# Mamba on one core: the products that add dt*u*B for half of TensorE's pairs of states become scalings on ScalarE and transposes

## What is computed

```python
xz = h @ in_proj_w
u, z = jnp.split(xz, 2, axis=-1)
u = silu(causal_depthwise_conv(u, conv_w, conv_b))
xdbl = u @ x_proj_w                      # dt_r, B, C
dt = softplus(dt_r @ dt_proj_w + dt_proj_b)
A = -jnp.exp(A_log)
def step(hst, inp):
    dt_t, B_t, C_t, u_t = inp
    dA = jnp.exp(dt_t[..., None] * A)
    dBu = dt_t[..., None] * B_t[:, None, :] * u_t[..., None]
    hst = dA * hst + dBu
    y = jnp.einsum('bdn,bn->bd', hst, C_t)
    return (hst, y)
y = (scanned y + u * D) * silu(z)
out = x + y @ out_proj_w
```

## Time and profile before

| | us |
|---|---|
| median of 3 runs | 2734.17 |
| lowest and highest run | 2731.04, 2740.05 |
| profiled execution | 2753.53 |
| its span | 2751.6 |
| busy in the span: PE, DVE, ACT, POOL | 2466.9, 2244.3, 1961.6, 1899.4 |

### The profile page before, as it was taken

How to read it: one execution, slowest core, us unless ns; L and a number is a source line. 1 busy time by engine, 2 the same in 40 slices (tenths; PEclk the granted TensorE clock), 3 DMA queues, 4 the chain that set the end, 5 groups by cost and what they waited for, 6 DMA issues and landing times. The chain is left out here.

```text
span 2751.6 us, 42267 instructions
## 1 busy us (share of the span) xinstructions
PE 2466.9 (90%) x15334; PEld 1916.0 (70%) x15334; DVE 2244.3 (82%) x2324; ACT 1961.6 (71%) x2841; POOL 1899.4 (69%) x1213
## 2 busy tenths in 40 slices
PE   5999998699698999999999999999999999977894
PEld 4888886566266767777677777776777777766563
DVE  6788886454189999899998998999999999997554
ACT  3656565266589788788787888978879889773562
POOL 1211212232289999999999998988989989897562
PEclk9999999799899999999999999999999999999897
DMA  1211212422323033041330421303303113051133
GB/s 53 65 50 50 64 46 79 99 78 66 91 86 112 29 127 122 21 132 51 97 120 21 134 82 51 124 10 115 117 9 124 67 58 116 21 166 46 61 105 127
DMA packets 143233, 219.62 MB, mean 80 GB/s; under 512 B 27076, under 2 KB 109892, under 8 KB 143044
## 3 DMA queue, kind: packets, MB, share of 16 engines
q1 hardware_dynamic: 134884, 194.84, 22.5%
q0 software_dynamic: 8160, 22.29, 2.9%
HBM read 174.56 MB, written 42.53 MB: 79 GB/s over the span
## 5 line engine op out<-in xcount | busy, mean ns | idle before, releaser
L1521 POOL TENSOR_TENSOR m_state<-m_state,m_c_all 128x1024 f32<-128x1024 f32 x512 | 1199.0, 2364 | 125.2 <-DVE m_state L1628 122.9
L1628 DVE TENSOR_TENSOR_SCAN m_state<-m_decay,m_ps_d 128x1024 f32<-128x1024 f32 x512 | 1152.0, 2274 | 92.1 <-ACT m_decay L1687 46.3
L1687 ACT ACTIVATE m_decay<-m_dt,m_aneg 128x511 f32<-128x511 f32 x1024 | 663.9, 709 | 20.1 <-DVE m_state L1628 19.4
L1965 PEld LDWEIGHTS m_ps_d<-m_bdiag,m_duT 128*128 128x128 f32 x4096 | 497.6, 194 | 96.3 <-issue 74.2
L1978 PE MATMUL m_ps_y<-k_ident,m_state 128*128 128x128 f32 x4096 | 521.0, 274 | 6.6 <-POOL m_state L1521 6.5
L1965 PE MATMUL m_ps_d<-m_bdiag,m_duT 128*128 128x128 f32 x4096 | 509.2, 278 | 17.0 <-DVE m_state L1628 16.4
L1978 PEld LDWEIGHTS m_ps_y<-k_ident,m_state 128*128 128x128 f32 x4096 | 468.4, 142 | 66.9 <-issue 55.8
L1616 DVE TENSOR_TENSOR m_ps_d<-m_ps_u,m_b_all 128x1024 f32<-128x1024 f32 x256 | 315.6, 1233 | 34.7 <-DMA m_b_all<-m_bc_rows 14.2
L1872 PE MATMUL m_ps_f<-k_w_2a,k_w_1b 128*128 128x512 f32 x512 | 255.8, 625 | 43.2 <-ACT m_up L1784 30.9
L1897 PE MATMUL m_ps_f<-m_up,k_w_1b 128*128 128x512 f32 x512 | 230.2, 592 | 0.7 <-ACT m_up L1784 0.7
L280 POOL TENSOR_TENSOR a_trig_lo<-a_trig,a_trig_hi 128x2048 fp32r<-128x2048 f32 x16 | 75.6, 4724 | 160.7 <-ACT a_trig_hi L561 160.7
(11 more groups left out here) (228 smaller groups left out, 4318.8 us busy)
## 6 DMA issues: line engine op xcount, KB each, us to landing
m_c_all<-m_bc_rows SPq DMA_DIRECT2D x128, 512.0 KB, 5.7
m_b_all<-m_bc_rows SPq DMA_DIRECT2D x64, 512.0 KB, 7.4
out<-m_xw SPq DMA_DIRECT2D x32, 512.0 KB, 3.3
a_w_2a<-x SPq DMA_DIRECT2D x16, 512.0 KB, 4.6
a_xres<-x SPq DMA_DIRECT2D x16, 512.0 KB, 5.4
x<-a_xout SPq DMA_DIRECT2D x16, 512.0 KB, 3.3
k_w_2a<-x SPq DMA_DIRECT2D x16, 512.0 KB
m_xw<-out SPq DMA_DIRECT2D x16, 512.0 KB, 8.6
```

The source lines that it names most:

```text
L1521: nc.gpsimd.tensor_tensor(s, s, c_all[:, n, :, :], ALU.mult).then_inc(weighed, 1)
L1628: nc.vector.tensor_tensor_scan(state[:, r, :, :].rearrange("p n t -> p (n t)"), decay[:, r, :, :].rearrange("p n t -> p (n t)"), ps_d[i % ...
L1687: ins = nc.scalar.activation(decay[:, r, j, 1:S], dt_sb[:, c % DR, 1:S], ACT.Exp, scale=aneg[:, c, n:n + 1])
L1965: ins = nc.tensor.matmul(ps_d[1][:, j, t * P:(t + 1) * P], duT[:, c % DR, t, :], bdiag[:, n // 2, TT * j + t, :], start=True, stop=True)
```

## The change

The drives of n = 5 and n = 7 are made in another way in all four channel blocks. ACT multiplies `duT`, with time on the partitions, by B of each time step (a scale per partition) into a new buffer `du_b`, one for each of the two n: eight instructions of 128 columns (`scale_duT`). PE transposes the eight tiles into `ps_d[1]`. The table `SCALED` says at which unit of ACT's list which block (c, n) is made. The diagonal blocks of n = 5 (POOL) and n = 7 (ACT) are no longer made; `bdiag` has two pairs instead of four. The drives of n = 1 and 3 stay.

```diff
+    SCALED = {2: (0, 5), 4: (0, 7), 9: (1, 5), 11: (1, 7), 14: (2, 5), 16: (2, 7), 22: (3, 5), 24: (3, 7)}
...
-        bdiag = sb("bdiag", [P, NP // 2, 2 * TT, P])
+        bdiag = sb("bdiag", [P, 2, 2 * TT, P])
+        du_b = [sb(f"du_b{m}", [P, 2 * TT, P]) for m in range(2)]
...
-        b_made = [sem(f"b_made{m}") for m in range(NP // 2)]
+        b_made = [sem(f"b_made{m}") for m in range(2)]
+        du_b_ready = [sem(f"du_b_ready{m}") for m in range(2)]
...
-                    if i == 0 and st.has(0):
-                        diagonal(st, 0, 5)
...
-            def diagonal(st, o, n):
-
-                h, b = st.half(o), st.item(o)
+            def scale_duT(st, c, n):
+
+                h, b, m = st.half(0), st.item(0), n // 2 - 2
                 act.wait_ge(bt_ready, b + 1)
-                if st.has(o - 1):
-                    act.wait_ge(drive_full, UN // 2 * b - NP // 2 + n // 2 + 1)
+                act.wait_ge(duT_ready, CT * b + c + 1)
+                if c or st.has(-1):
+                    act.wait_ge(drive_full, UN // 2 * b + (NP * c + n) // 2 + 1 - NP // 2)
                 for j in range(2):
                     for t in range(TT):
-                        ins = nc.scalar.activation(bdiag[:, n // 2, TT * j + t, :], id_sb[:, :], ACT.Copy,
+                        ins = nc.scalar.activation(du_b[m][:, TT * j + t, :], duT[:, c % DR, t, :], ACT.Copy,
                                                    scale=bt[h][:, 2 * n + j, t:t + 1])
-                ins.then_inc(b_made[n // 2], 1)
+                ins.then_inc(du_b_ready[m], 1)
...
-                    if i == 4 and st.has(0):
-                        diagonal(st, 0, 7)
+                    if i in SCALED and st.has(0):
+                        scale_duT(st, *SCALED[i])
...
-                if c == 0:
+                if c == 0 and n < 4:
                     pe.wait_ge(b_made[n // 2], b + 1)
+                if n > 4:
+                    pe.wait_ge(du_b_ready[n // 2 - 2], CT * b + c + 1)
                 if i >= 2 or st.has(o - 1):
                     pe.wait_ge(scanned, UN * b + i - 1)
                 for j in range(2):
                     for t in range(TT):
-                        ins = nc.tensor.matmul(ps_d[1][:, j, t * P:(t + 1) * P], duT[:, c % DR, t, :],
-                                               bdiag[:, n // 2, TT * j + t, :], start=True, stop=True)
+                        if n > 4:
+                            ins = nc.tensor.transpose(ps_d[1][:, j, t * P:(t + 1) * P],
+                                                      du_b[n // 2 - 2][:, TT * j + t, :], id_sb[:, :])
+                        else:
+                            ins = nc.tensor.matmul(ps_d[1][:, j, t * P:(t + 1) * P], duT[:, c % DR, t, :],
+                                                   bdiag[:, n // 2, TT * j + t, :], start=True, stop=True)
```

## The result

The changed kernel takes 2807.2 us (median of 4 runs, 2805.64 to 2811.95) beside 2734.06 of the kernel before: ratio 1.0269 [1.0253, 1.0286], 73 us slower. The forecast was 2747, and 2807 lies outside its range of 2712 to 2780. The profiled execution took 2806.57 us. Before's lay 19 us above its median, and what lies outside the marks of the Mamba items explains it (2753.53 - 1666.68 = 1086.9 us, against 1065.1 in the change), so the comparison is made by these marks.

A forecast was written before the change was run, and what follows sets the result against it. DVE was tightest, PE late, ACT had 17.7 us room per item; the change makes ACT the bound. Steps of +8.8, -1.2 and +7.5 us, with -2 in the last item, give +13 on 2734.2: 2747 us, range 2712 to 2780.

The forecast's parts named there:

- The costs of the operations: Per item: ACT blocks 2.34 us each, seven more make 16.4; transposing drives 0.89 instead of 1.78, saving PE 7.1.
- The wait for x: ACT's wait of 3.2 us per item for the projection x was to be gone.
- DVE's waits for decays: DVE's scans waiting for ACT's decays: up from 2 to 4 us or more, a sign the forecast is right.
- GpSimd's lost block: POOL's diagonal block of 1901 ns per item goes; worth nothing by itself, as POOL soon waits for a scan.
- the walk of the blocks through the item: New ACT blocks laid into a late item with old durations and order: the cycle ends at 116.1 instead of 115.57.
- 108.3 busy + 0.3 + 0.15 + 1.65 waits = 110.4: Check of a late item's period: ACT's busy time plus its remaining waits, 1.65 of them for the fourth convolution.
- my last rival: Drives still take 1.78 us, ACT has 16.4 us more, convolutions come as late as now: 2787 us, chance 0.03.
- The stretch behind the next item's du: PE waits 3.1 us for z's silu, then runs at half clock: 1.35 us later on PE, +0.9 per item.
- The rival of a second stretch: PE idle at the third channel block's du slows the third and fourth convolutions, 1.7 us per item: 2772, chance 0.12.
- a gap need not be followed by a low stretch: Earlier trace: PE idles 3 us, clock stays 1.00; supports the rival that the clock does no harm, 2734, chance 0.20.
- that rival: Transposes don't hold the clock: 40 on PE at half speed reach z's silu 3.4 us later: 2797, chance 0.05.

The follow-up runs named there:

- e1: The change with one ScalarE block per item, read by all eight transposing drives, the other seven blocks left out: 2675.8 us, ratio 0.9784 to the kernel before.
- e2: The kernel before plus seven unread blocks of scalings per item on ScalarE at the change's units, products unchanged: 2870.8 us, ratio 1.0495.
- e9: The change plus filler on TensorE, 20 zero transposes ahead of the next item's du and 8 ahead of the fourth channel block's: 2799.2 us.
- e18: The change for the seventh pair only, blocks at units 4, 13, between third and fourth convolutions' silus, and 24; fifth pair as before, no filler: 2722.9 us.
- e16: e18 plus filler of 16 zero transposes ahead of the next item's du and 4 ahead of the fourth channel block's: 2702.5 us, ratio 0.9872 to before.
- e15: The kernel before plus three unread ScalarE blocks per item inside waits, at unit 13 and two between third and fourth convolutions' silus: 2739.6 us, ratio 1.0006.

## Why the prediction was wrong

**The costs of the operations were nearly right.** A block is 2.34 us and ACT 107.85 busy in a late item (forecast 108.3); a transposing drive has eight entries and 0.88 us to the next start (2189.44 to 2190.32; forecast 0.89), so twice as fast, where the rule of the Trainium skill (page "TensorE: Matmul & The Clock Gate", Terms) has four times; the trace decides. The wait for x is gone, DVE's waits for decays grew, as said. PE is busy 101.7 us in the late item where I had 97.3: part of it is the low clock, and 98.65 in a late item of e1, at 1.00, leaves 1.35 open. That GpSimd's lost block is worth nothing was not tried by itself.

**The step that failed is the walk of the blocks through the item**, with its check "108.3 busy + 0.3 + 0.15 + 1.65 waits = 110.4". Measured beside the 107.85: 3.22 for the fourth convolution (1.65), 1.75 for B (none), 1.07 for z ("is gone"; I gave 0.9 back by the clock), 0.57 for the second convolution (0.3), 6.97 us of waits in all. So a late item took 115.5 us instead of 111.2, and the first ten 116.5 instead of 112.9. I moved the convolutions earlier by what PE's drives save and let ACT's delays run on through DVE alone. They also run through the PSUM banks that PE takes over from ACT's up and x copies and DVE's gate, and through POOL's du, which waits for the softplus. So the work that ACT waits for came later with ACT. The same error stands in my last rival: ACT's load without relief was priced at 2787, 53 above before; e2 measured 136.

**The clock.** The stretch behind the next item's du came as forecast: a gap of 3.52 us (3.1), then 0.50. The rival of a second stretch came true too, at another place: not at the du of the third channel block but at that of the fourth, behind waits of 1.23 and 1.60. I gave it 0.12 and 2772, on top of a walk that was already short. Both stretches together cost 1.5 us of a late item (115.5 beside 114.0 in e9), so the 0.9 that I gave the first one was of the right size, if the two are alike. That a gap need not be followed by a low stretch, as in the earlier trace rows, is so too: e18 has both answers at one place.

**Transposes and the clock.** Sixteen transposes of zeros as filler leave the granted clock at 1.00 in e16, in all fifteen items, at a place where it falls to 0.50 in eight items of e18. By the rule of the Trainium skill (same page, Part 4: transposes don't count as PE being busy in the same way) they should not have; that rival is refuted here.

**The range** took in the unknown durations, which were known well, and hardly the walk, which was not. The walk of four coupled engines was 4 us per item off, 60 in all, and the range gave it nothing of its own. What each of the waits adds is shown only in sum; how the cost of blocks 22 and 24 splits stays open, since their later places brought waits of their own.

## What to carry to other kernels

An engine's waits in a fixed order are sure room only at the place where it waits: work put ahead of them can delay what it feeds, and the awaited result moves along. How much depends on the place: here three blocks ahead of the waits cost 13 us of their 112, seven 136 of their 262. Before adding work, ask of each wait whether what is awaited was itself fed by this engine, and put the work behind the last thing that feeds it; three blocks cost nothing that could be measured inside the waits, and half the change there, with filler, made a faster kernel. Price both halves of a trade apart by two runs (relief alone, load alone): here they added up to within 4 us.

## What was not expected of the hardware

PE got more work (20 to 32 zero transposes per item) and the kernel got 8 to 20 us faster, because the granted clock stayed at 1.00 where in many items it had fallen to 0.50 behind an idle stretch of 2.7 us or more (2.66 to 3.58 in e18, beside e16; in the other pairs part of the low stretches stayed). And a Copy with a scale between two silus costs no table load: in e15 sixteen of them stand between the silus at 2135.61 and 2141.46, with none in the row.
